# Audio tower on one core: the first norm's rows are made ahead of the routing, and a score is masked ahead of a masked product

## The chip, the cores and the metric

The kernel runs on one core of a Trainium2 chip. The metric is the device time of one execution in microseconds (us). The core has five engines that run beside each other, each through its own instructions in the order of the program, and wait for each other by semaphores: TensorE (PE, matmuls and transposes), VectorE (DVE), ScalarE (ACT), GpSimd (POOL) and SyncE (SP), which here only issues DMAs. PEld in the profile is TensorE's weight load.

## The reference

The input x is 16 batches of 375 rows of 256. Three layers follow, the second and third with a residual:

```python
h = gelu(x[:, 1:] @ W[:D] + x[:, :1] @ W[D:] + b)              # token layer: 374 rows per batch
h = h + attn(layernorm(h))                                     # cosine attention
h = h + ffn(layernorm(h))                                      # routed attention, 8 experts

def attn(x):      # softmax over (x_i . x_j) / (|x_i||x_j|), then the sum over x, plus x
def ffn(x):
    logits = (x/|x|) @ (sim/|sim|) - sigmoid(gates)            # 8 experts
    mask   = logits > 0, or the two best where none is
    rw     = softmax(relu(logits) where mask)
    q, k, v = einsum('tc,ecd,te->td', x, proj, mask)           # D = 128
    o      = causal_softmax(q @ k.T / sqrt(D)) @ v
    return einsum('td,edc,te->tc', o, o_proj, mask * rw)
```

## The kernel before

**Tiling.** The 374 rows of a batch are three tiles of 128 rows (NT = 3, the last with 118). Precision is kept by splitting a float32 into a high and a low float16 and adding three products (high·high, high·low, low·high): `split_product` (L1820 is its matmul). A unit `M(k)` of TensorE is one expert's masked product for q, v or k: 24 units a batch (0 to 7 q, 8 to 15 v, 16 to 23 k), six matmuls of 374 columns each.

**Stages.** A head (to about 72 us) runs the token layer of all batches and the first attention of the first two. Then `pipeline` calls `step(i, g, f, m, n)` on each engine, for i = 1 to 17. In a step, batch m is in its q/v/k products, batch n = m-1 in scores, softmax, heads and output pairs, batch f = m+1 in the cosine attention and the routing, and batch g (g1 in three of the engines) = f+1 in its first norm. Step 1 (`early(m)`, m = 0, no n yet) is the head's last step; steps 2 to 14 have all four; step 15 has no g1; steps 16 and 17 are the end. The order of each engine is written out by hand in `step`, five times. A step of 2 to 14 takes 39.3 us.

**The first norm's path.** DVE: `norm_stats(0, g1)`. POOL: `norm_rows(0, g1)` and `row_scales(g1)`, small chains on three columns (L662 is the scale). DVE: `norm_apply(0, g1)`, three tiles of scaled rows `xs` (L1290). ACT: `high_1(g1)`, two copies of all of it to float16 (L886 `xhl`, L887 `xh_sum`). POOL: `low_1(g1)`, the low part (L709). SP: `first_rows_around(g)`, one transposing DMA into `xT` (L461), behind waits for high and low. TensorE: `dots(g, t)`, the dot products of the next step.

**The routing's path.** TensorE `logits(f)` between units 14 and 15, DVE `route(f)` (from L1364, 16 small operations, to the two that write the mask, L1393 and L1394), TensorE `turn_mask(f)` (L1908) behind unit 17, ACT `turned_mask(f)` (L953), SP `mask_around(f)`: to DRAM and back over all partitions as `mask_all`, DVE `mask_tokens(f, e)` (L1407). POOL computes the routing weights beside it (`route_weights`, L725 to L734).

**The output pairs.** TensorE makes 12 products `pair(n, p)` of two experts each, in two banks by turns. ACT scales the right half of each (`scale_pairs`, L1033), then DVE adds the left half into h (`add_pair`, in `step` as `pairs(a, b)`, L1312, which waits for ACT's scaling of the same pair). Pair p of TensorE waits until pair p-2 is added.

**The scores.** TensorE `score(n, 0..2)` uses two banks: `score(n, 2)` waits until DVE's `mask_scores(n, 0)` (L1488) has read the first. `turn_exp(f)` (L1871) transposes blocks of the cosine exponentials and waits for `exp_low(f, 1)` (L1428); `exp_lower(f)` (L1437) copies them out; `attend(f, t)` (L1884 to L1888) needs both. DVE's `mask_tokens(m, 5)` makes the input of unit `M(5)`.

```python
M(4); turn_exp(f); score(n, 2); M(5); attend(f, 0..2)          # TensorE, steps 2 to 15
exp_low(f, 1); mask_tokens(m, 5); mask_scores(n, 0); mask_scores(n, 1)   # DVE
```

Of the kernel before, what the change touches and what calls it, by code (L numbers as in the profile page):

```python
# [26 lines left out]
def audio_tower_kernel(nc, x, tok_w, tok_b, sim_matrix, gates, q_proj, k_proj, v_proj, o_proj, out):  # L27
# [7 lines left out]
    PAIRS = NT * E // 2  # L35
# [11 lines left out]
    with ExitStack() as ctx:  # L47
# [297 lines left out]
        def early(m):  # L345

            return isinstance(m, int) and m == 0
# [60 lines left out]
        def _(sp):  # L408
# [35 lines left out]
            def norms_out(g):  # L444

                sp.wait_ge(s_rnorm1, g + 1).then_inc(s_passed, 1)
                sp.dma_start(d_rnorm[g, :].rearrange("(p t) -> p t", p=P), small[0][:, 5, :]).then_inc(s_rn_stored, 16)

            def norms_in(g):

                sp.wait_ge(s_rn_stored, 16 * (g + 1)).then_inc(s_passed, 1)
                if later(g):
                    sp.wait_ge(s_cos_ready, NT * g).then_inc(s_passed, 1)
                sp.dma_start(rnorm_row[:, :], d_rnorm[g, :].partition_broadcast(P)).then_inc(s_rn_loaded, 16)

            def first_rows_around(g):

                sp.wait_ge(s_hi1, 2 * (g + 1)).then_inc(s_passed, 1)
                sp.wait_ge(s_lo1, g + 1).then_inc(s_passed, 1)
                sp.wait_ge(s_dots_done, NT * g).then_inc(s_passed, 1)  # L460
                sp.dma_start_transpose(xT[0][:, :, :, :].rearrange("p a c (t q) -> p (a c t) q", q=P),  # L461
                                       xhl[0][:, :, :, :, :].rearrange("p a c t q -> p (a c t q)")).then_inc(s_T1_moved, 16)
# [114 lines left out]
            def step(i, g, f, m, n):  # L577
                if n is not None and by_trip(n):
                    probs_around(n)
                if early(m):  # L580
                    load_output_weights()
                    mask_around(f)
                if f is not None and not early(m):
                    second_rows_around(f)
                if g is not None:
                    norms_out(g)
                    norms_in(g)
                if f is not None and not early(m):
                    mask_around(f)
                if m is not None and by_trip(m):  # L590
                    values_out(m)
                if g is not None:
                    first_rows_around(g)
                if m is not None and by_trip(m):
                    values_in(m)
                if final(m):
                    route_around()
                if final(n):
                    last_stores(n)
                elif n is not None:  # L600
                    for t in range(NT - 1 if final(m) else NT):
                        store(n, t)
# [5 lines left out]
        def _(pool):  # L608
# [95 lines left out]
            def low_1(b):  # L704

                pool.wait_ge(s_hi1, 2 * b + 1).then_inc(s_passed, 1)
                if later(b):
                    pool.wait_ge(s_att_done, NT * b).then_inc(s_passed, 1)
                g.tensor_tensor(xhl[0][:, 1, :, :, :], xs[0][:, :, :, :], xhl[0][:, 0, :, :, :],  # L709
                                ALU.subtract).then_inc(s_lo1, 1)  # L710
# [79 lines left out]
            def step(i, g1, f, m, n):  # L790
                if n is not None and not final(n):
                    low_probs(n)
                    if by_trip(n):
                        values_low(n)
                if f is not None and not early(m):
                    norm_rows(1, f, LN_SCALE ** 4, NORM_EPS * NORM_EPS)
                if g1 is not None:
                    norm_rows(0, g1, 1.0, 1e-38)
                    row_scales(g1)
                if f is not None:  # L800
                    route_weights(f)
                if early(m):
                    low_1(g1)
                if final(n):
                    pool.wait_ge(s_tile_summed, 2 * NT * n).then_inc(s_passed, 1)
                    sum_products(n, 0)
                    add_sum(n - 1, NT - 1)
                    pool.wait_ge(s_tile_ready, NT * n).then_inc(s_passed, 1)
                    sum_halves(n, 0)
                elif n is not None:  # L810
                    sum_products(n, 0)
                    if g1 is not None:
                        low_1(g1)
                    sum_halves(n, 0)
                    add_sum(n, 0)
                if n is not None and not final(n):
                    add_tile(n, 1)
                    if final(m):
                        low_probs(m)
                        sum_products(n, 2)  # L820
                        weighted_rest(1)
                        sum_halves(n, 2)
                    else:
                        add_tile(n, 2)
# [16 lines left out]
        def _(act):  # L841
# [177 lines left out]
            def step(i, g1, f, m, n):  # L1019
# [24 lines left out]
                if early(m):  # L1044
                    weights_high(2 * NC - 1)
                    turned_rows_2(f)
                    weights_high(2 * NC)
                    weights_high(2 * NC + 1)
                    head_high(qT, qkv_bank[0], s_q_done, m + 1, s_q_hi, [], qkv_out)
                    turned_mask(f)  # L1050
                    route_exp(f)
                    values_out(m)
                    high_1(g1)
                    output_weights_high(0)
                    output_weights_high(1)
                    high_k()
                    return
# [29 lines left out]
                    head_high(qT, qkv_bank[0], s_q_done, m + 1, s_q_hi,  # L1087
                              [(s_scores_done, NT * m)] if later(m) else [], qkv_out)
                if f is not None and n is not None:
                    scale_pairs(0, 5)  # L1090
                    turned_mask(f)
                    if by_trip(m):
                        values_out(m)
                    else:
                        high_k()
                    route_exp(f)
                    scale_pairs(5, 7)
                    if g1 is not None:
                        high_1(g1)
                    scale_pairs(7, PAIRS)  # L1100
                    if by_trip(m):
                        high_k()
                    else:
                        high_v()
                    return
# [78 lines left out]
        def _(dve):  # L1184
# [334 lines left out]
            def step(i, g1, f, m, n):  # L1519
# [9 lines left out]
                if early(m):  # L1529
                    for e in range(3, E):  # L1530
                        mask_tokens(m, e)
                    dve.wait_ge(s_xm_ready, E * f)
                    turned_low_2(f)
                    weights_low(2 * NC - 1)
                    dve.wait_ge(s_h_ready, B)
                    v.memset(v_out[:, T:TP], 0.0)
                    norm_stats(0, g1)
                    route(f)
                    weights_low(2 * NC)
                    head_low(qT, qkv_bank[0], s_q_hi, m + 1, s_q_lo, qkv_out)  # L1540
                    weights_low(2 * NC + 1)
                    weight_max(f)
                    weight_sum(f)
                    turn_values(m)
                    norm_apply(0, g1)
                    for e in range(E - 4):
                        mask_tokens(f, e)
                        if e in (1, 3):
                            output_weights_low(e // 2)
                    cosines(g1, 0)  # L1550
                    head_low(kT, qkv_bank[1], s_k_hi, m + 1, s_k_lo, qkv_out)
                    cosines(g1, 1)
                    mask_tokens(f, E - 4)
                    return
                if n is not None and f is not None:
                    exp_low(f, 0)
                    cosines(f, 2)
                    exp_low(f, 1)
                    mask_tokens(m, E - 3)
                    mask_scores(n, 0, out_bank[0])  # L1560
                    mask_scores(n, 1, out_bank[1])
                    exp_low(f, 2)
                    exp_lower(f)
# [9 lines left out]
                                    ALU.mult).then_inc(s_sum2_s, 1)  # L1573
                    low_2(f)
                    output_weights(n)
                    head_low(qT, qkv_bank[0], s_q_hi, m + 1, s_q_lo, qkv_out)
                    pairs(0, 3)
                    route(f)
                    pairs(3, 4)
                    weight_max(f)  # L1580
# [3 lines left out]
                        head_low(kT, qkv_bank[1], s_k_hi, m + 1, s_k_lo, qkv_out)  # L1584
                    pairs(4, 5)
                    weight_sum(f)
                    if g1 is not None:
                        norm_scaled(0, g1)
                        norm_apply_tile(0, g1, 0)
                    pairs(5, 6)  # L1590
                    if g1 is not None:
                        norm_apply_tile(0, g1, 1)
                        norm_apply_tile(0, g1, 2)
                    pairs(6, 7)
                    pairs(7, 8)
                    for e in range(E - 4):
                        pairs(8 + e, min(9 + e, PAIRS))
# [606 lines left out]
```

## Time and profile before

| | |
|---|---|
| runs shown, median (range) | 700.22 us (698.68 to 700.27) |
| the profiled execution, its own time | 699.35 us |
| its span in the trace | 697.6 us |
| granted TensorE clock, mean | 0.998 of full |
| TensorE busy | 681.4 us, 98% |
| DVE busy | 546.7 us, 78% |
| POOL busy | 405.8 us, 58% |
| ACT busy | 345.4 us, 50% |

The profiled execution's time is 1.75 us over its span and 0.87 us under the median. TensorE is nearly always busy, so what counts is the idle time of TensorE and what ends it. On the page the mean of a matmul is its latency; in the views in order of time, the start of a group less the start of the group before it is the time that the group before held TensorE (six matmuls of 374 columns are 0.95 us from start to start and are shown as 1.11 us long).

### The profile page before, as it was taken

What the parts mean: (1) busy time and instruction counts of PE and PEld (TensorE: products, weight loads), DVE (VectorE), ACT (ScalarE), POOL (GpSimd) and SP (SyncE); (2) the same over time, 40 slices, a digit from 0 to 9 for tenths busy, and PEclk for the clock granted to TensorE, in tenths of its full rate; (3) what the DMA queues carried; (4) which work ended last, traced back from release to release, by engine and by line L of the source; (5) the groups of instructions that cost most, each with busy time, mean ns of one, the idle gap of its engine ahead of it and who ended that gap; (6) DMA issues with size and microseconds to landing.
All of it is one profiled execution on the core that took longest, in us unless ns stands there. A gap on an engine that the chain in (4) does not pass through costs nothing.

```text
span 697.6 us, 17459 instructions
## 1 busy us (share of the span) xinstructions
PE 681.4 (98%) x4856; PEld 435.9 (62%) x4856; DVE 546.7 (78%) x1428; ACT 345.4 (50%) x768; POOL 405.8 (58%) x669
## 2 busy tenths in 40 slices
PE   9999989999999999999999999999999999999998
PEld 8887656565655656565655656565655656565555
DVE  5778868786979788796979788796979788786636
ACT  5977444444536354444636354444636354453443
POOL 7552325665747676565747676565747676563534
PEclk9999999999999999999999999999999999999999
DMA  9671142424324252423334242423334242422121
GB/s 247 161 183 50 62 103 43 107 53 90 69 50 112 49 117 49 103 54 87 67 53 112 49 117 46 106 54 86 66 55 112 49 117 45 107 57 68 24 75 31
DMA packets 128310, 57.29 MB, mean 82 GB/s; under 512 B 100264, under 2 KB 124056, under 8 KB 128152
## 3 DMA queue, kind: packets, MB, share of 16 engines
q1 hardware_dynamic: 127888, 56.60, 35.0%
q10 hardware_dynamic: 392, 0.32, 0.1%
q8 instruction: 15, 0.25, 0.1%
q14 instruction: 15, 0.12, 0.1%
HBM read 30.45 MB, written 9.01 MB: 57 GB/s over the span
## 4 chain that ended last, share of the span: by engine, by line
PE 81%; DVE 6%; issue 5%; POOL 3%; DMA 2%; ACT 2%; DVEq 0%; POOLq 0%; ACTq 0%; SPq 0%
PE bank L1820 70%; PE bank L1884 2%; PE bank L1888 2%; PE bank L1886 2%; DVE xm L1407 2%; PE bank L1740 2%; PE bank L1729 1%; DMA mask_all<-d_mask 1%; DMA xT<-xhl 1%; DVE region_b L1290 1%; DMA region_b<-in_x_dram 1%; DVE exp_hl L1428 1%; DVE region_a L1488 1%; POOL small L660 0%; DVE xinT L1211 0%
## 5 line engine op out<-in xcount | busy, mean ns | idle before, releaser
L1820 PE MATMUL bank<-xm,w_qkv 128*128 128x374 f16 x2304 | 409.6, 323 | 0.0
L1820 PEld LDWEIGHTS bank<-xm,w_qkv 128*128 128x128 f16 x2304 | 223.4, 98 | 146.8 <-issue 0.6
L1033 ACT ACTIVATE region_c<-bank,out_w 128x256 f32<-128x256 f32 x180 | 83.3, 473 | 159.1 <-PE bank L1820 142.4
L1820 PE MATMUL bank<-w_o,aoT 128*128 128x512 f16 x540 | 143.1, 379 | 0.4
L1407 DVE TENSOR_TENSOR xm<-xT,mask_all 128x1496 f16<-128x1496 f16 x128 | 139.5, 1103 | 1.5 <-DMA mask_all<-d_mask 1.3
L1312 DVE SCALAR_TENSOR_TENSOR h<-bank,out_w,h 128x256 f32 (+1 forms) x180 | 85.9, 477 | 47.5 <-ACT region_c L1033 45.2
L748 POOL TENSOR_TENSOR region_c<-region_c 128x512 f32<-128x512 f32 x46 | 68.7, 1493 | 25.4 <-ACT region_c L1033 20.5
L787 POOL TENSOR_TENSOR exp_hl<-exp,exp_hl 128x128 f16<-128x128 f32 (+2 forms) x48 | 50.5, 1053 | 56.4 <-ACT exp_hl L976 54.3
L1820 PEld LDWEIGHTS bank<-w_o,aoT 128*128 128x128 f16 x540 | 49.2, 98 | 51.4 <-DVE h L1312 12.9
L755 POOL TENSOR_TENSOR region_c<-region_c 128x256 f32<-128x256 f32 x46 | 47.6, 1034 | 5.8 <-POOL region_c L748 5.5
L902 ACT ACTIVATE aoT<-bank 128x374 f16<-128x374 f32 x15 | 7.2, 483 | 87.7 <-PE bank L1820 87.7
L762 POOL TENSOR_TENSOR h<-region_c,h 128x256 f32 (+1 forms) x45 | 41.2, 917 | 15.2 <-POOL region_c L755 15.2
L1290 DVE TENSOR_SCALAR region_b<-h,moments,small 128x256 f32 (+1 forms) x96 | 35.1, 410 | 12.4 <-POOL small L662 12.4
L926 ACT ACTIVATE region_a<-region_a,log_p,small 128x374 f32<-128x374 f32 (+2 forms) x48 | 28.3, 590 | 28.0 <-DVE region_a L1418 28.0
L1820 PE MATMUL bank<-xT 128*128 128x374 f16 (+2 forms) x288 | 38.4, 271 | 2.4 <-DMA xT<-xhl 2.4
L1884 PE MATMUL bank<-xh_sum,exp_hl 128*128 128x257 f16 x144 | 39.5, 274 | 0.0
L1888 PE MATMUL bank<-xh_sum,exp_hl 128*128 128x257 f16 x144 | 39.2, 272 | 0.0
L1886 PE MATMUL bank<-xhl,exp_hl 128*128 128x256 f16 x144 | 39.0, 271 | 0.0
L1740 PE MATMUL bank<-w_tok,xinT 128*128 128x256 f16 x288 | 37.6, 273 | 0.7 <-ACT h L865 0.7
L1273 DVE BATCH_NORM_STATS2 stats<-h 128x6 f32 (+1 forms) x96 | 35.8, 415 | 0.0
L725 POOL TENSOR_TENSOR lg<-lg 128x24 f32<-128x24 f32 x16 | 4.6, 287 | 52.8 <-DVE lg L1394 52.8
L1820 PEld LDWEIGHTS bank<-xT 128*128 128x128 f16 x288 | 25.4, 99 | 12.9 <-DMA xT<-xhl 2.8
(211 smaller groups left out, 1026.1 us busy)
## 6 DMA issues: line engine op xcount, KB each, us to landing
mask_all<-d_mask SPq DMA_DIRECT2D x32, 384.0 KB, 4.3
h<-in_x_dram SPq DMA_DIRECT2D x16, 256.0 KB, 4.9
out_dram<-h SPq DMA_DIRECT2D x31, 128.0 KB
rnorm_row<-d_rnorm SPq DMA_DIRECT2D x16, 192.0 KB, 3.6
d_v<-xinT SPq DMA_DIRECT2D x14, 192.0 KB, 4.4
xinT<-d_v SPq DMA_DIRECT2D x56, 48.0 KB, 2.3
h<-in_x_dram SPq DMA_DIRECT2D x15, 112.0 KB, 5.6
out_dram<-h SPq DMA_DIRECT2D x15, 112.0 KB
```

The source lines that it names most:

```text
L748: g.tensor_tensor(prod_sum[:, 0:2, :], prod[:, buf, 0:2, :], prod[:, buf, 2:4, :], ALU.add).then_inc(s_tile_summed, 1)
L755: g.tensor_tensor(prod_sum[:, 2, :], prod_sum[:, 0, :], prod_sum[:, 1, :], ALU.add).then_inc(s_tile_summed, 1)
L787: done = g.tensor_tensor(probs_tile(1, i), full, probs_tile(0, i), ALU.subtract)
L1033: a.activation(prod[:, prod_buf(n, t), q, :], pair_bank(n, p)[:, C:2 * C], ACT.Copy, scale=weights_out(n)[:, t, 2 * q + 1:2 * q + 2]).then ...
L1290: v.tensor_scalar(xs[n][:, :, t, :], h[:, b, t, :].rearrange("p (c q) -> p c q", c=NC), moments[n][:, t, 0:1], small[n][:, 4, t:t + 1], AL ...
L1312: v.scalar_tensor_tensor(h[:, n, t, :], pair_bank(n, p)[:, 0:C], weights_out(n)[:, t, e0:e0 + 1], h[:, n, t, :], ALU.mult, ALU.add).then_i ...
L1407: v.tensor_tensor(xm[:, e, :, 0:T], xT[1][:, :, :, 0:T].rearrange("p a c t -> p (a c) t"), mask_all[:, e, 0:T].unsqueeze(1).broadcast_to([ ...
L1740: t_.matmul(projected(t), xinT[:, b % 2, xp, c, t * P:(t + 1) * P], w_tok[:, wp, c, :], start=(c == 0 and xp == 0 and wp == 0), stop=False ...
L1820: last = t_.matmul(dst, left[lp], right[rp], start=(starts and k == 0), stop=(stops and k == 2), skip_group_check=True)
L1884: t_.matmul(banks[t][:, 0:C + 1], high, xh_sum[:, j, 0:C + 1], start=(j == 0), stop=False, skip_group_check=True)
L1886: t_.matmul(banks[t][:, 0:C].rearrange("p (c q) -> p c q", c=NC), high, xhl[0][:, 1, :, j, :], start=False, stop=False, skip_group_check=True)
L1888: last = t_.matmul(banks[t][:, 0:C + 1], low, xh_sum[:, j, 0:C + 1], start=False, stop=(j == NT - 1), skip_group_check=True)
```

## The change

Four engines get another order; nothing is computed otherwise.

- Step 1: DVE's `norm_apply(0, g1)` goes right behind `route(f)`; ACT's `high_1(g1)` ahead of `turned_mask`; POOL's `low_1(g1)` ahead of `route_weights`; SP's `first_rows_around(g)` between `norms_out` and `norms_in`.
- Steps 2 to 14: DVE adds pair 0, then makes `head_low(qT)`, then all three tiles of `norm_apply(0, g1)`, then adds pairs 1 and 2, then `route(f)`; ACT's `high_1(g1)` stands behind the scaling of pairs 0 and 1 and ahead of those of pairs 2 to 4; POOL's `low_1(g1)` ahead of `route_weights(f)`; SP's `first_rows_around(g)` behind `norms_in` and ahead of `mask_around`.
- Steps 2 to 15: DVE's `mask_scores(n, 0)` ahead of `mask_tokens(m, 5)`.

```diff
@@ SP step
                 if g is not None:
                     norms_out(g)
+                    if early(m):
+                        first_rows_around(g)
                     norms_in(g)
+                    if not early(m):
+                        first_rows_around(g)
                 if f is not None and not early(m):
                     mask_around(f)
                 if m is not None and by_trip(m):
                     values_out(m)
-                if g is not None:
-                    first_rows_around(g)
@@ POOL step
                     row_scales(g1)
+                    low_1(g1)
                 if f is not None:
                     route_weights(f)
-                if early(m):
-                    low_1(g1)
...
                     sum_products(n, 0)
-                    if g1 is not None:
-                        low_1(g1)
                     sum_halves(n, 0)
@@ ACT step, early
                     head_high(qT, qkv_bank[0], s_q_done, m + 1, s_q_hi, [], qkv_out)
+                    high_1(g1)
                     turned_mask(f)
                     route_exp(f)
                     values_out(m)
-                    high_1(g1)
@@ ACT step
-                    scale_pairs(0, 5)
+                    scale_pairs(0, 2)
+                    if g1 is not None:
+                        high_1(g1)
+                    scale_pairs(2, 5)
                     turned_mask(f)
...
                     route_exp(f)
-                    scale_pairs(5, 7)
-                    if g1 is not None:
-                        high_1(g1)
-                    scale_pairs(7, PAIRS)
+                    scale_pairs(5, PAIRS)
@@ DVE step, early
                     route(f)
+                    norm_apply(0, g1)
                     weights_low(2 * NC)
...
                     turn_values(m)
-                    norm_apply(0, g1)
@@ DVE step
                     exp_low(f, 1)
+                    mask_scores(n, 0, out_bank[0])
                     mask_tokens(m, E - 3)
-                    mask_scores(n, 0, out_bank[0])
                     mask_scores(n, 1, out_bank[1])
...
                     output_weights(n)
+                    pairs(0, 1)
                     head_low(qT, qkv_bank[0], s_q_hi, m + 1, s_q_lo, qkv_out)
-                    pairs(0, 3)
+                    if g1 is not None:
+                        norm_apply(0, g1)
+                    pairs(1, 3)
                     route(f)
...
                     weight_sum(f)
-                    if g1 is not None:
-                        norm_scaled(0, g1)
-                        norm_apply_tile(0, g1, 0)
-                    pairs(5, 6)
-                    if g1 is not None:
-                        norm_apply_tile(0, g1, 1)
-                        norm_apply_tile(0, g1, 2)
-                    pairs(6, 7)
+                    pairs(5, 7)
                     pairs(7, 8)
```

## Rows read from the trace of the kernel before

**Rows 1.** The page, busy time and its share of the span, TensorE.

```profile
PE 681.4 (98%) x4856; PEld 435.9 (62%) x4856; DVE 546.7 (78%) x1428; ACT 345.4 (50%) x768; POOL 405.8 (58%) x669
```

**Rows 2.** Waits over the run: waiter <- releaser: us, times, longest.

```profile
PEld bank L1820 <- DVE row_max L1488: 10.1, 14, 0.8
```

**Rows 3.** TensorE in order of time, one step: start, length, operation, idle before.

```profile
263.09 0.50 PE L1871 MATMUL bank<-ident,exp_hl 128*128 128x128 f16 x6
264.14 0.66 PE L1820 MATMUL bank<-kT,qT 128*128 128x384 f16 x3 [0.55 <-DVE row_max L1488]
...
265.59 0.27 PE L1884 MATMUL bank<-xh_sum,exp_hl 128*128 128x257 f16 x1
```

**Rows 4.** DVE in order of time, the same stretch; the last row later.

```profile
262.30 0.73 DVE L1428 TENSOR_TENSOR exp_hl<-region_a,exp_hl 128x246 f16<-128x246 f32 x1
262.95 0.92 DVE L1407 TENSOR_TENSOR xm<-xT,mask_all 128x1496 f16<-128x1496 f16 x1
263.80 0.28 DVE L1488 CUSTOM_DVE_ANT_0 region_a<-bank,causal 128x128 f32<-128x128 f32 x1
...
264.55 0.61 DVE L1437 COPY exp_hl<-bank 128x256 f16<-128x256 f16 x2
...
294.79 1.61 DVE L1407 TENSOR_TENSOR xm<-xT,mask_all 128x1496 f16<-128x1496 f16 x1
```

**Rows 5.** TensorE in order of time: pair 3 and the turning of the mask.

```profile
280.55 0.81 PE L1820 MATMUL bank<-w_o,aoT 128*128 128x512 f16 x3
...
284.70 0.33 PE L1908 MATMUL bank<-ident,mask 128*128 128x128 f16 x3
```

**Rows 6.** DVE in order of time, from q's low part to the mask.

```profile
277.29 0.55 DVE L1301 SCALAR_TENSOR_TENSOR qT<-bank,qT 128x374 f16<-128x374 f32 x1
278.06 1.08 DVE L1312 SCALAR_TENSOR_TENSOR h<-bank,out_w,h 128x256 f32 x2 [0.22 <-ACT region_c L1033]
279.97 0.48 DVE L1312 SCALAR_TENSOR_TENSOR h<-bank,out_w,h 128x256 f32 x1 [0.82 <-ACT region_c L1033]
280.73 0.21 DVE L1364 COPY logit_parts<-bank 128x48 f32<-128x48 f32 x1 [0.28 <-PE bank L1900]
...
284.09 0.18 DVE L1393 TENSOR_TENSOR mask<-lg 128x24 f16<-128x24 f32 x1
```

**Rows 7.** ACT in order of time: the scaling of pair 2, and high_1.

```profile
279.46 0.47 ACT L1033 ACTIVATE region_c<-bank,out_w 128x256 f32<-128x256 f32 x1 [1.19 <-PE bank L1820]
...
288.85 0.84 ACT L886 ACTIVATE xhl<-region_b 128x768 f16<-128x768 f32 x1
289.60 0.83 ACT L887 ACTIVATE xh_sum<-region_b 128x768 f16<-128x768 f32 x1
```

**Rows 8.** POOL in order of time: the first norm's scale, and low_1.

```profile
276.75 0.25 POOL L662 TENSOR_SCALAR small<-small 128x3 f32<-128x3 f32 x1 [0.20 <-POOL small L660]
...
289.97 1.65 POOL L709 TENSOR_TENSOR xhl<-region_b,xhl 128x768 f16<-128x768 f32 x1
```

**Rows 9.** TensorE, pairs 6 and 7: a step with g1, and step 15 without.

```profile
287.41 1.62 PE L1820 MATMUL bank<-w_o,aoT 128*128 128x512 f16 x6
...
640.82 1.46 PE L1820 MATMUL bank<-w_o,aoT 128*128 128x512 f16 x6
```

**Rows 10.** Step 1 and its end, in order of time; the last row is of the windows view.

```profile
82.89 0.18 DVE L1394 TENSOR_TENSOR lg<-lg 128x24 f32<-128x24 f32 x1
...
90.10 1.02 DVE L1290 TENSOR_SCALAR region_b<-h,moments,small 128x256 f32<-128x256 f32 x3
...
92.27 2.27 POOL L709 TENSOR_TENSOR xhl<-region_b,xhl 128x768 f16<-128x768 f32 x1 [1.71 <-ACT xhl L886]
...
94.70 1.86 SPq L461 DMA_TRANSPOSE xT<-xhl  x1
...
99.19 1.12 PE L1820 MATMUL bank<-xT 128*128 128x374 f16 x6 [2.42 <-DMA xT<-xhl]
...
100.00:105.00 5.00, 5.00 (x29) 3.06 (x28) 2.92 (x5) 2.37 (x4) 0.00 (x0) 0.66 0.20 32
```

The columns of that last row are: stretch and its length; busy us and count of PE, PEld, DVE, ACT and POOL; granted TensorE clock; DMA share; GB/s.

## The prediction

> **What bounds the kernel now.** The page comes first: TensorE is busy for 98% of the span [rows 1], so the time is its work plus its gaps, and an edit that only changes orders can win no more than the gaps. The views in order of time of the four engines come next, for one step of the 13 that are alike (2 to 14), and then for step 1. Adding up TensorE's starts in that step leaves four gaps that count, 1.1 us of 39.3: 0.7 before the third score [rows 3], 0.2 before pair 2, 0.16 inside pairs 6 and 7 [rows 9], and a few hundredths elsewhere. In step 1 there is one large gap, 2.42 us, in which the first dot products wait for the transposing DMA, with a lower clock behind it [rows 10].
>
> **Step 1: the first norm's rows.** Now the rows are scaled at 90.10, made low at 92.27 to 94.54, and the transposes are issued at 94.70 and have landed when TensorE goes on at 99.19, 4.5 us later [rows 10]. After the change DVE scales them right behind the routing's last operation at 82.89, to about 84.0; ACT's two copies, 1.6 us [rows 7], end by 85.7, while it would be waiting for the mask. POOL comes to `low_1` at about 87.2, when its chain of small operations is through, and needs 2.3 us [rows 10]. The issue is then at about 89.6 and the landing at 94 by the 4.5 us of now. Bounds: the mask's loads are in the DMA engines then, so the landing may be as late as 98. TensorE wants the rows at 96.6. I take the whole gap as gone, 2.4 us and 0.2 more for the drain of the matmuls ahead, since 94 has 2.6 us of room; the lower bound is 1.2.
>
> Behind the gap the granted clock was 0.66 over 5 us [rows 10]: it stood at the lower of its two levels, 1.2 instead of 2.4 GHz, for most of it, right after TensorE had been idle for 2.4 us. That cost 5 × 0.34 = 1.7 us, and goes with the gap (kept at worst: 0).
>
> Beside it: POOL's routing weights start 2.3 us later, so DVE's `weight_max`, `weight_sum` and `turn_values` do too, and `mask_tokens(f, 0)` starts about 1.1 us later (the 1.0 us of row scaling has gone from ahead of it). DVE had 2 us of idle time before the first cosines, since they waited for the late dot products, and this is what hides it. SP's issue (1.9 us) passes only `norms_in`, whose own wait for the stored norms is longer. Step 1: **-4.3 us** (bounds -1.2 and -4.5).
>
> **The score masked first, steps 3 to 15.** TensorE's transposes at 263.09 hold it for 0.33 us, to 263.42; the third score starts at 264.14, when `mask_scores(n, 0)` has read its bank: a gap of 0.72 [rows 3]. DVE ran exp_low to 263.0, the masked product for unit 5 (262.95, 0.92 long) and the masked score at 263.80 [rows 4]. With the order turned, the score is masked from 262.95 to about 263.25, ahead of 263.42, and the third score doesn't wait. But what is late next? The masked product now ends at 262.95 + 0.21 + 0.92 = 264.1. TensorE would want it at 263.42 + 0.50 = 263.92 (three matmuls of 384 columns, 0.66 less the 0.16 of drain), so unit 5 waits 0.2 us and ends at 265.1. Then `attend` needs `exp_lower`, which ends at 264.55 + 0.61 = 265.16 in either order, because DVE has no idle time in between and its total is the same. So `attend` starts at 265.22 instead of 265.59 [rows 3, 4]: a gain of 0.37, about half of the gap. The waits view has 14 waits of this kind [rows 2]; one is step 16's, where the order is such already, so 13 × 0.37 = **-4.8 us** (bounds 0 and -0.72 each: 0 to -9.4).
>
> **The norm moved ahead of the routing, steps 2 to 14.** This is where I expect the loss. The scale is there in time: L662 ends at 277.0 [rows 8]. DVE: pair 0 is added at 278.06 as now (it waits for ACT), q's low part follows (0.55 us, moved out of what was idle time), then three tiles of rows, 1.02 to 1.06 us, from about 278.9 to 280.0 [rows 6, 10]. ACT has scaled pairs 0 and 1 and stands at `high_1`, waiting for all three tiles. It makes its two copies from 280.03, the second 0.75 behind the first, and the next operation follows 0.74 behind that [rows 7]: pair 2 is scaled from 281.52 to 282.0. Now it is scaled from 279.46 [rows 7]. So the scaling of pair 2, which TensorE had ready at 279.4, stands 2.06 us behind work that nobody needs soon.
>
> Behind it on DVE: pair 1 is added at 279.9 (in time for TensorE's pair 3 at 280.55 [rows 5], with 0.1 us to spare), then DVE waits for pair 2, adds it at 282.03, and `route(f)` begins at 282.43 instead of 280.73 [rows 6]. The routing waits only because it stands behind that add: its logits are ready at 280.7. Delay 1.70 us. From its first operation to the end of L1393 and L1394 it takes 3.6 us [rows 6], so the mask is there at about 286.0. TensorE turns the mask at 284.70 [rows 5], and now has some 0.3 us of room, since the mask is written by 284.37. So TensorE stands still until about 286.1: a new gap of **1.42 us** in each of 13 steps, 18.5 us. Bounds: nothing at all if the delay were under 0.3 us; 1.9 us if the routing's operations get longer as well.
>
> Given back: without the row scaling between pairs 4 and 5, DVE adds pair 5 by 0.3 us earlier relative to TensorE, so the 0.16 us inside pairs 6 and 7 goes. Step 15, which has no first norm, shows it: 1.46 us against 1.62 [rows 9]. I take 0.15 × 13 = **-2.0 us** (bounds 0 and -2.1). ACT's 1.6 us of copies no longer delay pairs 6 and 7 around 289 to 290, but TensorE's pairs 8 and 9 weren't waiting on those.
>
> **At nothing.** POOL: `low_1` (1.65 us [rows 8]) runs when POOL would wait for the mask; with the routing late it is through before. SP: the transposes pass `mask_around` in the queue, which waits for ACT's `turned_mask`; issued at about 283.2, they are off the queue by 284.7, ahead of the mask's row. The mask's way through DRAM hangs on TensorE's turning, so it shifts with TensorE and costs nothing more; DVE's tail (four masked products, pairs 8 to 11, cosines) is set by the pairs and by the dot products, so it doesn't either. If these covers were gone, a masked product late by x costs x a step.
>
> **The sum.** -4.3 - 4.8 + 18.5 - 2.0 = +7.4 us. On the profiled execution's own 699.35 us this is 706.8; its median of runs lies 0.87 higher. I put the forecast at **707.2 us**, about 1% slower.
>
> **A rule of the Trainium skill.** The row first: a masked product took 0.92 us with POOL idle and 1.61 us beside POOL's sums [rows 4]. The Trainium skill, "GPSIMD Engine Reference", section "1. Specifications", says that GpSimd's way to SBUF is shared with VectorE, with contention for VectorE instructions that read two SBUF tensors. This speaks against the change, and the two mask rows agree with it: `low_1` is moved from beside pair adds, which read one operand from a bank, to beside the start of the routing, which reads two from SBUF.
>
> **The rivals.**
> - *A, the forecast*, 707.2: the new gap at the turning of the mask outweighs the others. For it: three of its four links are queue orders, and the delay of 1.70 us is five times the room. Own range 701 to 713.
> - *B, the gap is given back*: TensorE later in the step finds everything ready that it now waits for, 1.1 us in all. Then a step costs 1.42 - 1.1 = 0.3 us and the total is 699.35 + 4.2 - 4.3 = about 699.5, no difference. Against it: the gap before the third score is made by DVE work that starts from TensorE's own dot products shortly before, and moves with them.
> - *C, faster*: the copies on ACT don't hold the routing, because I misread where DVE is free. Then only gains remain: -4.3 - 4.8 - 2.0 = -11.1, about 688.7. It would need the rows scaled about 1.7 us earlier than I have them, before pair 0 is added.
> - *D, the clock*: after 2.4 us of idle time TensorE's clock fell and cost 1.7 us; after 0.72 us it never did. 1.42 us lies between. If each new gap sets it off, 13 × 1.7 = 22 us more: 729.
> - *E, the shared way*: beside `low_1` (281.5 to 283.1) about 1.1 us of pair 2's add and the routing would run slower by 1.61/0.92, which loses 0.47 us a step, 6.1 us: 713.3. Against it: the operations of the routing are short, and mostly fixed cost.
>
> **How the numbers follow.** A 0.63, B 0.12, C 0.10, D 0.07, E 0.08. The range leaves out C and D: 697.5 to 714.5, which takes in A's own range and E. A measurement can tell about 0.3%, 2.1 us, from no change. Faster by more than this: C and a small part of B's scatter, 0.12. Within: the rest of B, 0.10. Slower: 0.78.
>
> **What would show it.** In the changed profile: ACT's L886 and L887 stand between the second and third L1033 of a step, at about 280 to 281.6 in this step's times; DVE shows some 1.7 us of idle time before the add of pair 2, released by ACT L1033; TensorE waits about 1.4 us before L1908, released by DVE's mask (L1393), 13 times; the third score no longer waits for row_max but unit 5 waits about 0.2 us for xm; pairs 6 and 7 take 1.46 us; in step 1 the wait for xT is gone and the clock stays up. A step takes 40.2 us instead of 39.3. The prediction is wrong if L1908 doesn't wait, or if the clock falls behind it.

## The result, and the profile after

The changed kernel takes 728.37 us (median of 4 runs, 727.81 to 729.62) against 699.45 us before: a ratio of 1.042, interval 1.039 to 1.044. The forecast was 707.2 us with a range to 714.5. The direction was right and the size was not: +28.9 us instead of the +7.4 of the sum. One of the five executions of e6 below took 876.36 us at a mean granted clock of 0.754 and is left out of its ratio; without it the median of e6 is 695.75 us.

The page of the kernel after, first its busy time [rows 1 before]:

```profile
span 727.9 us, 17447 instructions
PE 685.8 (94%) x4856; PEld 437.6 (60%) x4856; DVE 554.2 (76%) x1428; ACT 341.9 (47%) x768; POOL 399.1 (55%) x669
```

TensorE does the same work in a span 30.3 us longer, 94% busy instead of 98%. Its waits (waiter <- releaser: us in total, times, longest):

```profile
PEld bank L1903 <- DVE lg L1393: 38.0, 13, 3.1
PEld bank L1815 <- DVE h L1311: 7.8, 21, 0.8
PEld bank L1815 <- DVE h L1446: 4.3, 12, 0.4
PEld bank L1815 <- DVE row_max L1487: 0.8, 1, 0.8
```

L1903 is the turning of the mask, L1393 the end of the routing: 13 waits, as forecast: 11 with 2.67 to 2.69 us of idle time, and two, in steps 2 and 3, with 1.8. The wait for row_max [rows 2] is gone but for step 16's, and a small one for the residual (L1446) is new. TensorE in order of time, the same places of one step as in rows 3, 5 and 9:

```profile
268.86 0.50 PE L1866 MATMUL bank<-ident,exp_hl 128*128 128x128 f16 x6
269.20 0.65 PE L1815 MATMUL bank<-kT,qT 128*128 128x384 f16 x3
269.69 1.11 PE L1815 MATMUL bank<-xm,w_qkv 128*128 128x374 f16 x6
270.65 0.28 PE L1879 MATMUL bank<-xh_sum,exp_hl 128*128 128x257 f16 x1
...
289.07 1.11 PE L1815 MATMUL bank<-xm,w_qkv 128*128 128x374 f16 x6
292.86 0.34 PE L1903 MATMUL bank<-ident,mask 128*128 128x128 f16 x3 [2.67 <-DVE lg L1393]
...
295.59 1.46 PE L1815 MATMUL bank<-w_o,aoT 128*128 128x512 f16 x6
```

The third score starts at once (269.20), pairs 6 and 7 take 1.46 us, and unit 17 at 289.07 is followed by the mask at 292.86: 3.79 less the 0.95 that the unit takes, a gap of 2.84 us where I had worked out 1.42.

What stands behind it, on ACT, DVE and POOL [rows 6 to 8]:

```profile
285.37 0.84 ACT L885 ACTIVATE xhl<-region_b 128x768 f16<-128x768 f32 x1 [1.83 <-DVE region_b L1289]
286.12 0.83 ACT L886 ACTIVATE xh_sum<-region_b 128x768 f16<-128x768 f32 x1
286.85 0.82 ACT L1032 ACTIVATE region_c<-bank,out_w 128x256 f32<-128x256 f32 x2
...
287.33 0.48 DVE L1311 SCALAR_TENSOR_TENSOR h<-bank,out_w,h 128x256 f32 x1 [1.61 <-ACT region_c L1032]
287.74 0.20 DVE L1363 COPY logit_parts<-bank 128x48 f32<-128x48 f32 x1
287.96 1.63 DVE L1366 TENSOR_TENSOR lg<-logit_parts 128x24 f32<-128x24 f32 x1
289.63 0.18 DVE L1368 TENSOR_TENSOR lg<-lg,small 128x24 f32<-128x24 f32 x1
...
287.92 1.64 POOL L711 TENSOR_TENSOR xhl<-region_b,xhl 128x768 f16<-128x768 f32 x1
```

The queue part is as forecast: ACT's two copies stand ahead of the scaling of pair 2, and DVE is idle for 1.61 us for it. What I didn't have is the routing's first add, L1366. It adds 24 elements a partition and took 0.18 to 0.21 us in the steps of the kernel before; here it takes 1.63 us. It starts at 287.96, 0.04 us after POOL's `low_1` (L711, 287.92), and the next operation starts 0.07 us after `low_1`'s end. It is held for the whole of POOL's instruction.

A third part is the clock. From one start of `turn_exp` on TensorE to the next, steps 3 on take 39.3 us before. After, they take 41.3 to 41.6 us, and four of them 43.2 us. Behind the gap in these four the granted clock is at the lower level of 1.2 GHz (0.66 over 5 us in each, and 1.00 over 5 us behind the others); the windows view of one of them (stretch, length, busy us and count of PE, PEld, DVE, ACT, POOL, then the granted clock, DMA share, GB/s):

```profile
208.00:210.00 2.00, 1.71 (x10) 0.98 (x11) 1.09 (x5) 0.84 (x2) 0.82 (x4) 0.80 0.60 134
210.00:212.00 2.00, 2.00 (x7) 0.91 (x6) 1.28 (x5) 0.70 (x2) 0.55 (x3) 0.50 0.03 8
212.00:214.00 2.00, 2.00 (x11) 0.90 (x9) 0.12 (x1) 0.46 (x1) 1.61 (x2) 0.84 0.75 206
214.00:216.00 2.00, 2.00 (x13) 1.16 (x12) 0.97 (x2) 0.62 (x3) 1.64 (x3) 1.00 0.73 281
```

Step 1 did what was forecast: the first dot products start at 96.46 instead of 99.19 [rows 10], with the clock at 1.00, and by the transposes of step 2 TensorE is 4.4 us ahead: 4.3 in step 1, and 0.1 from the head, where nothing was changed.

```profile
85.06 11.56 PE L1815 MATMUL bank<-xm,w_qkv 128*128 128x374 f16 x72
96.46 1.11 PE L1815 MATMUL bank<-xT 128*128 128x374 f16 x6
```

The account of the 30.3 us of span: step 1 -4.4; from step 2 to step 3 +2.0; the 12 steps behind it +33.1, of which 4 × 1.7 = 6.8 is clock and 12 × 2.2 = 26.3 is the gaps, less what the rest of a step gives back; the remainder is -0.4.

### The profile page after: what moved, and what is told of

The parts are those of the page before. It is cut to its first block, busy times and chain, and to the rows that moved or that the text cites. A ratio compares the mean times of both kernels' runs of the same rounds, so it can differ in the third digit from the quotient of the medians.

```text
span 727.9 us, 17447 instructions
## 1 busy us (share of the span) xinstructions
PE 685.8 (94%) x4856; PEld 437.6 (60%) x4856; DVE 554.2 (76%) x1428; ACT 341.9 (47%) x768; POOL 399.1 (55%) x669
## 4 chain that ended last, share of the span: by engine, by line
PE 65%; DVE 16%; issue 6%; ACT 6%; DMA 3%; SPq 1%; POOL 1%; DVEq 1%; ACTq 0%; POOLq 0%
PE bank L1815 54%; DVE lg L1366 3%; PE bank L1735 2%; PE bank L1879 2%; DVE region_b L1289 2%; PE bank L1883 2%; PE bank L1881 2%; ACT region_c L1032 2%; DVE xhl L1463 2%; ACT xhl L895 2%; DVE h L1311 1%; ACT xh_sum L886 1%; DMA xm<-in_L_ffn_q_proj_dram 1%; PE bank L1724 1%; DMA mask_all<-d_mask 1%
## 5 line engine op out<-in xcount | busy, mean ns | idle before, releaser
L1815 PE MATMUL bank<-xm,w_qkv 128*128 128x374 f16 x2304 | 414.3, 324 | 0.2
L750 POOL TENSOR_TENSOR region_c<-region_c 128x512 f32<-128x512 f32 x46 | 70.7, 1538 | 32.6 <-ACT region_c L1032 27.7
L1815 PEld LDWEIGHTS bank<-w_o,aoT 128*128 128x128 f16 x540 | 51.5, 99 | 51.2 <-DVE h L1311 7.6
L789 POOL TENSOR_TENSOR exp_hl<-exp,exp_hl 128x128 f16<-128x128 f32 (+2 forms) x48 | 37.5, 782 | 73.2 <-ACT exp_hl L975 73.1
L757 POOL TENSOR_TENSOR region_c<-region_c 128x256 f32<-128x256 f32 x46 | 44.1, 959 | 8.1 <-POOL region_c L750 7.8
L1883 PE MATMUL bank<-xh_sum,exp_hl 128*128 128x257 f16 x144 | 39.3, 273 | 0.0
L662 POOL TENSOR_TENSOR small<-small,m_half 128x3 f32<-128x3 f32 x32 | 35.9, 1120 | 5.9 <-POOL small L660 5.9
L1903 PE MATMUL bank<-ident,mask 128*128 128x128 f16 x48 | 5.4, 222 | 33.0 <-DVE lg L1393 33.0
```

Of the source, the lines that this page charges most:

```text
L750: g.tensor_tensor(prod_sum[:, 0:2, :], prod[:, buf, 0:2, :], prod[:, buf, 2:4, :], ALU.add).then_inc(s_tile_summed, 1)
L757: g.tensor_tensor(prod_sum[:, 2, :], prod_sum[:, 0, :], prod_sum[:, 1, :], ALU.add).then_inc(s_tile_summed, 1)
L1815: last = t_.matmul(dst, left[lp], right[rp], start=(starts and k == 0), stop=(stops and k == 2), skip_group_check=True)
L1883: last = t_.matmul(banks[t][:, 0:C + 1], low, xh_sum[:, j, 0:C + 1], start=False, stop=(j == NT - 1), skip_group_check=True)
```

## The experiments

Two theories stand against each other. **Two causes**: half of the new gap is queue order on ACT and DVE (1.4 us), half is that POOL's `low_1` keeps the add from going on, called the hold below (1.45 us). **Queues alone**: the order makes all of it, and the long add is only how the profile shows it.

### e1: low_1 late again

```diff
 # POOL, steps 2 to 14
                     row_scales(g1)
-                    low_1(g1)
+                    if early(m):
+                        low_1(g1)
...
                     sum_products(n, 0)
+                    if g1 is not None:
+                        low_1(g1)
                     sum_halves(n, 0)
```

SP's `first_rows_around(g)` goes back behind `values_out` with it.

> The changed kernel with POOL's low_1 (steps 2 to 14) back behind the first sum of products, and SP's transposes back behind the mask; ACT and DVE stay changed. Theory (two causes): the new gap of 2.84 us before the mask is turned is 1.4 us of queue order on ACT and 1.45 us in which a small VectorE operation of the routing is held until POOL's low_1 ends. Then the routing's first add is back at 0.18 us, the gap falls to 1.4 us, the clock no longer falls behind it, and the time is 728.4 - 13 x 1.45 - 6.8 = about 703 us. Rival (the queues alone make the gap): still about 728 us.

Measured: 710.40 us, ratio to the kernel before 1.017 (1.014 to 1.020). The add is back at 0.18 us and TensorE's gap at the mask is 286.71 less 284.37 and 0.95: 1.39 us, against the 1.42 of the prediction.

```profile
283.26 0.18 DVE L1369 TENSOR_TENSOR lg<-logit_parts 128x24 f32<-128x24 f32 x1
...
284.37 1.11 PE L1818 MATMUL bank<-xm,w_qkv 128*128 128x374 f16 x6
...
286.71 0.34 PE L1906 MATMUL bank<-ident,mask 128*128 128x128 f16 x3 [1.23 <-DVE lg L1396]
```

The clock is 1.000: it fell behind none of the 13 gaps (1.4 us, in steps 2 and 3 shorter). The time is 7 us over the 703 that I expected. A step takes 40.47 us, 0.4 more than the changed kernel's 41.55 less 1.45, which makes some 5 of the 7 us; e3, e5 and e10 show which waits these are. The first two holds were also shorter than 1.45, by 0.9 us together.

### e2: high_1 one place later

```diff
 # ACT, steps 2 to 14
-                    scale_pairs(0, 2)
+                    scale_pairs(0, 3)
                     if g1 is not None:
                         high_1(g1)
-                    scale_pairs(2, 5)
+                    scale_pairs(3, 5)
```

> The changed kernel with ACT's high_1 one place later, behind the scaling of pair 2; low_1 stays early. Two causes: the routing starts as in the kernel before (1.7 us earlier), but low_1 now starts in the middle of it and holds one of its operations for up to 1.5 us; a gap of about 1.1 us stays before the turning of the mask, about 728.4 - 13 x 1.7 - 6.8 = 699.5 us. Rival (queues alone): no gap, 728.4 - 13 x 2.84 - 6.8 = about 685 us.

Measured: 708.37 us, ratio 1.014 (1.011 to 1.016). The routing now starts in time, and there is still a gap, 1.21 us, so queues alone don't make it. The hold has moved to another operation, a comparison on three elements a partition (L1382, 0.17 us before), and again ends with `low_1`:

```profile
282.98 0.35 DVE L1379 TENSOR_TENSOR cmp<-cmp,lower 128x192 f32<-128x192 f32 x1
283.01 1.81 POOL L711 TENSOR_TENSOR xhl<-region_b,xhl 128x768 f16<-128x768 f32 x1
283.36 1.49 DVE L1382 TENSOR_SCALAR row<-row 128x3 f32<-128x3 f32 x1
```

`low_1` is itself longer by 0.17 us, as if it had first waited for the DVE operation that ran. The result is 9 us over the 699.5 expected. A step takes 40.25 us, where the changed kernel's 41.55 less 1.63 (its gap of 2.84 less this one) gives 39.92: the waits before unit 5 and `attend` of e1 are here too, and make some 4 of the 9 us. The rest is in part the smaller gap that I had assumed (1.1 us), and otherwise not accounted for.

### e3: both repairs

> Both edits: high_1 behind pair 2, low_1 and the transposes where they were. Both theories: no gap before the turning of the mask, the third score no longer waits, step 1 keeps its gain: about 685 us, faster than the kernel before by 2%.

Both edits together. Measured: 693.47 us, ratio 0.992 (0.989 to 0.995). The waits for the mask are gone, and this is faster than the kernel before, but by 5 us and not by 14. A step now takes 39.07 us against 39.28 before: with the two causes gone, and the clock's fall with them, no loss is left in steps 2 to 14, only a gain smaller than expected. TensorE's waits:

```profile
PEld bank L1818 <- DVE h L1314: 9.0, 26, 0.8
PEld bank L1818 <- DVE xm L1409: 5.9, 14, 0.4
PEld bank L1818 <- DVE h L1449: 5.0, 12, 0.4
PEld bank L1882 <- DVE exp_hl L1439: 3.8, 12, 0.3
```

The waits for xm (unit 5) and exp_hl (attend) are those that the prediction named. The 12 waits for the residual (L1449) are not. I had taken the changed kernel's step, where the third score, unit 5 and attend follow without a gap, as the measure; but there POOL's work lies elsewhere, because TensorE stood still. `exp_low(f, 1)` took 0.40 us there and takes 0.73 here, beside a POOL add. That alone isn't the reason: in e2 it takes 0.40 us too, and unit 5 still waits 0.22.

### e4: low_1 in three pieces

```diff
-                g.tensor_tensor(xhl[0][:, 1, :, :, :], xs[0][:, :, :, :], xhl[0][:, 0, :, :, :],
-                                ALU.subtract).then_inc(s_lo1, 1)
+                for t in range(NT):
+                    part_low = g.tensor_tensor(xhl[0][:, 1, :, t, :], xs[0][:, :, t, :], xhl[0][:, 0, :, t, :],
+                                               ALU.subtract)
+                part_low.then_inc(s_lo1, 1)
```

> The changed kernel with POOL's low_1 as three instructions of 128x256 instead of one of 128x768, at the same place. If VectorE's operation is held until the POOL instruction that runs ends: its first add takes at most 0.6 us instead of 1.63, though later operations of the routing may meet the next pieces; the gap falls by some 0.3 to 1 us and the time to 713 to 724 us. If POOL's traffic only slows VectorE, or the add waits for all of low_1: as long as now or longer, about 728 us or more.

Measured: 725.33 us, ratio 1.038 (1.035 to 1.040): 3 us less, just outside of the 713 to 724 that I expected. The view is more telling than the time:

```profile
288.69 1.93 POOL L712 TENSOR_TENSOR xhl<-region_b,xhl 128x256 f16<-128x256 f32 x3
288.73 0.67 DVE L1368 TENSOR_TENSOR lg<-logit_parts 128x24 f32<-128x24 f32 x1
289.43 0.60 DVE L1370 TENSOR_TENSOR lg<-lg,small 128x24 f32<-128x24 f32 x1
290.15 0.50 DVE L1374 TENSOR_TENSOR lg<-lg,sig 128x24 f32<-128x24 f32 x1
290.69 0.18 DVE L1376 TENSOR_SCALAR lg<-lg 128x24 f32<-128x24 f32 x1
```

One long hold became three short ones, one to each POOL instruction, and the total (1.23 us over the 0.18 each) is nearly what it was (1.45). So the hold lasts as long as the POOL instruction that runs, not as long as POOL has work: between two pieces one VectorE operation gets through. TensorE's gap is 2.62 us (idle time 2.45), and the clock still fell behind three of the 13 gaps, which is part of the time that stays.

### e5 to e7: the parts that gain, on the kernel before

e5 is the kernel before with the score masked first, e6 with the edits of step 1, e7 with both:

```diff
 # e5 and e7, DVE, steps 2 to 15
                     exp_low(f, 1)
+                    mask_scores(n, 0, out_bank[0])
                     mask_tokens(m, E - 3)
-                    mask_scores(n, 0, out_bank[0])
```

> The kernel before with only the score masked first (steps 2 to 15). By the prediction 0.37 us a step, 4.8 us in all: about 694 us. Rival, from the run with both repairs, where the gap before the third score went but waits of 0.22, 0.12 and 0.23 us came up behind it (unit 5, attend, the second residual): 0.15 us a step, about 2 us: 696.5 us.

> The kernel before with only the edits of step 1. Both theories: the wait for the transposes and the low clock behind it go, 4.4 us: about 694 us.

> The kernel before with both of these and the steps 2 to 14 otherwise as before. If the parts add: 698.6 - 4.4 - 2 to 4.8 = 689 to 692 us; it should be no slower than the run with both repairs (693.5), which still has the norm ahead of the routing on VectorE and ScalarE.

Measured: e5 695.21 us, ratio 0.994 (0.992 to 0.996); e6 696.04, 0.996 (0.993 to 0.998); e7 693.00, 0.991 (0.989 to 0.993). By the traces, a step of e5 takes 39.12 us instead of 39.28: 0.16 us, not 0.37. Up to `attend` the 0.37 is there, by e5's transposes and its first `attend`, 2.13 us apart where rows 3 have 2.50:

```profile
262.33 0.51 PE L1871 MATMUL bank<-ident,exp_hl 128*128 128x128 f16 x6
...
264.46 0.28 PE L1884 MATMUL bank<-xh_sum,exp_hl 128*128 128x257 f16 x1
```

0.21 of it is lost again behind, at the wait for the second residual (L1447, 12 times). e6 shows no gap and a full clock in step 1; its step 1 is 4.3 us shorter than before, of which 3.8 us are left at the transposes of step 2, since its head ran 0.5 us longer. In the traces the parts add: e7 has e6's step 1 (43.40 us) and e5's step (39.12). The medians don't quite, 6.4 us gained against 4.2 + 3.3, and e7 is 1 us over the 692 expected. The clock can make up the difference, since e5's four executions all have a mean clock of 0.999 or 1.000 and five of the eight before beside them have 0.997 or 0.998. e7 equals e3 in time. In e3 the norm ahead of the routing gives back 0.16 us at pairs 6 and 7, and loses 0.1 us that e8 finds.

### e8: q's low part first

```diff
 # DVE, e3's kernel, steps 2 to 15
+                    head_low(qT, qkv_bank[0], s_q_hi, m + 1, s_q_lo, qkv_out)
                     pairs(0, 1)
-                    head_low(qT, qkv_bank[0], s_q_hi, m + 1, s_q_lo, qkv_out)
```

> The kernel with both repairs, and on VectorE q's low part ahead of the add of pair 0 again. If the 0.1 us more before pair 2 (0.29 against 0.19) come from that order: 0.1 us a step, 1.3 us: about 692.2 us. If not: 693.5 us.

Measured: 691.24 us, ratio 0.989 (0.987 to 0.991). The gap before pair 2 is 0.19 again, a step takes 38.98 instead of 39.07. I had booked this move at nothing, as "moved out of what was idle time". With q's low part in front, DVE's add of pair 0 starts 0.63 us after ACT's scaling starts (e8; 0.62 in the kernel before); with DVE idle in front it is 0.73 (e3). Against e7, which has the norm where it was, a step of e8 is 0.14 us shorter and the time 1.8 us: once both repairs and this order are in, the norm ahead of the routing does gain, by what it gives back at pairs 6 and 7.

### e9 and e10: POOL waits for the masked products

```diff
 # POOL, low_probs
+                if not final(n):
+                    pool.wait_ge(s_xm_ready, E * (n + 2)).then_inc(s_passed, 1)
                 for i in range(NT):
                     pool.wait_ge(s_exp2_hi, NT * n + i + 1).then_inc(s_passed, 1)
```

e9 adds this to e8, e10 to e5.

> The fastest kernel so far (q's low part first, both repairs), with POOL's low halves of the probabilities waiting until VectorE's last masked products (6 and 7) are through, so that the two engines don't meet. If these products are long (2.25 us for two instead of 2.01) because POOL runs beside them, and this is what makes TensorE wait 0.22 us for the residual: they fall to about 1.9 us, the wait goes, and up to 0.22 x 13 = 2.9 us with it: 688.5 us. If the wait has another cause, or the later transposes come late for the next product: 691.2 us or more.

> The kernel before with only the score masked first, and the same wait on POOL. If the gain of the swap was halved (0.16 us a step instead of 0.37) by POOL's earlier start under the masked products: 0.37 us a step, 695.2 - 2.8 = 692.4 us. Otherwise 695.2 us or more.

DVE's masked products 6 and 7 (L1407, L1409) and POOL's low halves, in order of time, of e5 and then of e10:

```profile
264.80 2.25 DVE L1407 TENSOR_TENSOR xm<-xT,mask_all 128x1496 f16<-128x1496 f16 x2
265.22 1.04 POOL L787 TENSOR_TENSOR exp_hl<-exp,exp_hl 128x256 f16<-128x256 f32 x1 [0.82 <-ACT exp_hl L976]
```

```profile
263.00 1.77 DVE L1409 TENSOR_TENSOR xm<-xT,mask_all 128x1496 f16<-128x1496 f16 x2
265.12 1.93 POOL L789 TENSOR_TENSOR exp_hl<-exp,exp_hl 128x128 f16<-128x128 f32 x3 [4.91 <-DVE xm L1409]
```

Apart from each other, both are shorter: 1.77 instead of 2.25, and three POOL subtractions take 1.93 where they took 3.57 in the kernel before, from the first's start to the last's end. The wait for the residual is gone, and a step of e10 takes 38.90 us: 0.38 less than before, the 0.37 of the prediction. The span of the profiled run is 3.5 us shorter than e5's: 2.6 in the 12 steps from step 3 on, and 1.0 in the head, where nothing was changed. The timed runs show less: e10 694.52 us, ratio 0.995 (0.993 to 0.997), e9 690.53, 0.989 (0.987 to 0.990). Two of e10's five executions (695.99 and 696.43) have a mean clock of 0.997; the other three, at 1.000, take 693.01 to 694.52, against 694.75 to 696.57 for e5's four at 0.999 and 1.000. e9's step takes 38.77 us against e8's 38.98, but two of its first steps wait for transposed rows (idle 1.07 and 0.78 us) and are 1.2 and 0.6 us longer than e8's. So the cause of the short gain is shown in the step; its worth in the total is only indicated, by few executions at the same clock.

e8 and e9 beat both kernels, by 1.1% against the kernel before. Each still has the gaps before unit 5 (0.22) and attend (0.12).

## Why the prediction was wrong

**Step 1**: right. -4.3 forecast, 4.4 us ahead at step 2 in the changed kernel, clock included, and the later `mask_tokens` (1.45 us, not 1.1) was hidden as worked out. The 1.7 us of clock in it isn't lost in every execution of the kernel before. With the same gap in step 1, the profiled executions of e5 and e10 (idle 2.17 and 2.09 us) kept a clock of 1.00 and came through the step 1.9 and 2.0 us faster than the profiled one before. And of the 23 executions of the kernel before that were timed beside e1 to e10, 10 have a mean clock of 0.997 or 0.998 and take 698.91 to 700.12 us; the other 13, at 0.999 or 1.000, take 696.69 to 699.41.

**The score masked first**: the mechanism, the two waits left over (unit 5, attend) and the 0.37 us up to `attend` were right (e5), but the gain was half: 0.16 us a step, -2 us instead of -4.8. The step that failed is "a gain of 0.37", taken over the whole step as "13 × 0.37": I didn't ask what is late behind `attend`. The first score is masked 0.84 us earlier, so ACT and then POOL's first operation of `low_probs` start earlier, and POOL's operations fall otherwise on the masked products 6 and 7. These take 2.25 instead of 2.01 us for two, while TensorE comes 0.37 us earlier, and it waits 0.21 us for the second residual. e10 takes POOL away and gets 0.38.

**The norm ahead of the routing**: the queue term was right, 1.42 forecast and 1.39 measured in e1. The step that failed is the length put in behind it, "From its first operation to the end of L1393 and L1394 it takes 3.6 us". It takes 5.06 us when `low_1` starts beside it: 1.45 us more in each of 11 steps, 0.9 and 1.1 in the first two. I had put `low_1` under "at nothing", and that is where it should have been priced.

Rival E named the mechanism and gave it 0.47 us. Two things were wrong in that. The first is the law: it took the overlap to stretch work by 1.61/0.92. The rows show a hold until POOL's instruction ends. In steps 2 and 3 of the changed kernel the add starts 0.59 and 0.37 us after `low_1`, and it still ends 0.04 to 0.05 us after it:

```profile
120.45 1.64 POOL L711 TENSOR_TENSOR xhl<-region_b,xhl 128x768 f16<-128x768 f32 x1
121.04 1.10 DVE L1366 TENSOR_TENSOR lg<-logit_parts 128x24 f32<-128x24 f32 x1
...
161.79 1.64 POOL L711 TENSOR_TENSOR xhl<-region_b,xhl 128x768 f16<-128x768 f32 x1
162.16 1.31 DVE L1366 TENSOR_TENSOR lg<-logit_parts 128x24 f32<-128x24 f32 x1
```

The second is when `low_1` starts. I had it at 281.5 and the routing at 282.43, its first add 0.24 behind that, at 282.67. A hold from there to the end of `low_1` is only 0.3 us, so even the right law would have given less than 0.47. In the changed kernel `low_1` started 0.04 us before the add. It follows POOL's chain of small operations, and two of these were longer: a power, 1.51 instead of 0.88 us, held in its turn by DVE (shown at the end), and another (L674), 1.03 instead of 0.88 beside the scaling of the rows. The first comes with the other part of the change: the power takes 1.5 us in e5 and e7, which only mask the score first in these steps, and 0.88 in e6, which doesn't. The two are 0.78 us of the 1.13 by which `low_1` is nearer to the add than booked; the other 0.35 isn't traced. With 1.45 in the place of 0.47, rival E says 707.2 + 18.9 = 726.

**The clock**: rival D was right in part. Gaps of 1.4 us (e1) and 1.2 us (e2) never set it off, as forecast A had it. But the gap was 2.84, not 1.42, and then the clock fell behind four of the gaps in the profiled run, 1.7 us each, 6.8 us. The two small rivals weren't independent: what E names made the gap behind which D's fall came.

**Given back**: right in place and size, 0.16 us inside pairs 6 and 7. **q's low part**, booked at nothing, cost 0.1 us a step (e8).

**The sum with the measured terms**, on the span: -4.4 in step 1, 13 gaps of 2.84 less the first two's 0.9 each, +35.1, the third score's -0.72 × 13 = -9.4 (whole here, with no wait before unit 5 or `attend`; why they are missing in this kernel and not in e2 isn't settled), the residual's +0.21 × 12 = 2.5, pair 2's +0.1 × 13 = 1.3, pairs 6 and 7 -2.1, the clock +6.8: +29.8, against 30.3. The terms were measured first and then added, so this shows that nothing large is missing, and no more.

The Trainium skill, "SBUF — State Buffer", section "🔬 SBUF: two separate sides", says that the port pair which DVE and GpSimd share is locked for the full instruction by whichever starts first, and that the other blocks; on DVE's side this holds for operations with two SBUF inputs or in a 2-port mode. The traces agree: 1.63 us instead of 0.18 beside a POOL instruction of 1.64 us, and three holds beside three pieces. In the prediction I made a slowdown of it.

## What to carry to other kernels

Price a move by what it will run beside, on both VectorE and GpSimd: a 0.2 us operation that meets a GpSimd instruction can cost nearly that instruction's whole length (1.63 us here), and cutting the instruction up turned one hold into three (e4). Small shifts count: `low_1` started some 0.6 us later because a POOL operation was itself held, and that made the hold longer. In an in-order queue, look at what the moved block now stands in front of, and put it behind the last item that a critical engine waits for (here one pair further). A gain at one point of a step counts only if what stands behind it can also come earlier: take each operation there at both of its lengths, alone and beside the neighbour.

## What the runs showed of the hardware

- The hold hits very small operations: 24 elements, 0.18 to 1.63 us; three elements with one SBUF input (a comparison with a constant), 0.17 to 1.49 us (e2). Adds with one operand in a bank and one in SBUF weren't held beside `low_1` in the kernel before (1.02 us for two at 290.82, 1.08 for two elsewhere).
- It works the other way too: a POOL power on three elements, 0.88 us, took 1.51 us when it started 0.19 us behind DVE's 0.96 us subtraction of two SBUF tensors, in the changed kernel; in the kernel before it started 0.21 us ahead of it and took 0.88. The changed kernel, then the kernel before:

```profile
281.15 0.96 DVE L1463 TENSOR_TENSOR xhl<-region_b,xhl 128x768 f16<-128x768 f32 x1 [0.20 <-ACT xhl L895]
...
281.34 1.51 POOL L662 TENSOR_TENSOR small<-small,m_half 128x3 f32<-128x3 f32 x1 [0.18 <-POOL small L660]
```

```profile
275.68 0.88 POOL L660 TENSOR_TENSOR small<-small,m_half 128x3 f32<-128x3 f32 x1 [0.18 <-POOL small L658]
...
275.89 0.96 DVE L1464 TENSOR_TENSOR xhl<-region_b,xhl 128x768 f16<-128x768 f32 x1 [0.21 <-ACT xhl L896]
```

- In the profiled executions the clock fell behind 4 of the 11 gaps of TensorE of 2.84 us (idle time 2.67 to 2.69 in the row) and neither of the two with 1.8 in the changed kernel; in e4 behind one of 2.15 us of idle time and two of the 11 with 2.45; in step 1 behind 2.42 (kernel before) and not behind 2.17 (e5) or 2.09 (e10); and behind none of the 13 gaps of e1 or of e2, 1.24 us of idle time at most. Each fall in the changed kernel was some 3.4 us at the lower level (in the window rows above, 0.80, 0.50 and 0.84 over 2 us each). What picks the ones behind which it falls isn't settled.
